# A graph network of three attention layers and an MLP layer: chunks of edges laid out by sixteen to a partition, turned on VectorE

## The reference, cut to what matters

```python
def _gat(x, edge_index, W, att_s, att_d, bias, heads, ch, neg_slope):
    h = (x @ W.T).reshape(n, heads, ch)
    a_s = (h * att_s[None]).sum(-1)
    a_d = (h * att_d[None]).sum(-1)
    logits = leaky_relu(a_s[src] + a_d[dst], neg_slope)
    m = segment_max(logits, dst)
    ex = exp(logits - m[dst])
    denom = segment_sum(ex, dst)
    alpha = ex / (denom[dst] + 1e-16)
    out = segment_sum(alpha[:, :, None] * h[src], dst)
    return out.reshape(n, heads * ch) + bias
# x = layernorm(x + gat3(elu_clip(gat2(elu_clip(gat1(x))))))
# the MLP layer:
    e_feat = concatenate([x[src], x[dst], edge_attr], axis=-1)
    v = relu(e_feat @ W1 + b1) @ W2 + b2
    x_cand = segment_max(v, dst)
# x = layernorm(x + maximum(x_cand, x))
```

## Time and profile before

| | |
|---|---|
| device time, median of 3 runs | 19831.58 us (19803.22 to 19836.53) |
| span of the profiled execution | 18272.2 us, 130521 instructions |
| that execution's time beyond its span | not given separately |
| busy in the span: PE, PEld | 8944.7 us (49%), 5685.5 us (31%) |
| busy: DVE, ACT, POOL | 6628.1 us (36%), 2818.0 us (15%), 13988.6 us (77%) |
| DMA | 655.33 MB, 36 GB/s over the span |

### The profile page before, as it was taken

The page is one execution under the profiler, slowest core; times in us unless marked ns, Lnnn a source line. Parts: engine busy times, 40 slices in busy tenths (PEclk is TensorE's granted clock), DMA queues, the critical chain, the costliest instruction groups (busy, mean ns, idle before and its releaser), DMA issues. The chain is left out here.

```text
span 18272.2 us, 130521 instructions
## 1 busy us (share of the span) xinstructions
PE 8944.7 (49%) x27930; PEld 5685.5 (31%) x27930; DVE 6628.1 (36%) x8375; ACT 2818.0 (15%) x6155; POOL 13988.6 (77%) x13430
## 2 busy tenths in 40 slices
PE   2444444444244444444424444444442566666664
PEld 1333333333133333333313333333331222222221
DVE  3444444344344444443434444444444211111113
ACT  3111111111111111111111111111111111111111
POOL 6777777777777777777777777777777777777776
PEclk9999999999999999999999999999999777777776
DMA  3111111111111111111111111111111222222221
GB/s 97 37 39 37 38 39 38 38 37 39 22 26 26 26 26 26 26 26 26 26 19 26 26 26 26 26 26 26 26 26 23 50 53 52 52 53 53 53 53 41
DMA packets 1418083, 655.33 MB, mean 36 GB/s; under 512 B 575697, under 2 KB 1396834, under 8 KB 1417732
## 3 DMA queue, kind: packets, MB, share of 16 engines
q1 hardware_dynamic: 984610, 414.51, 8.3%
q0 software_dynamic: 433440, 240.48, 7.5%
HBM read 361.76 MB, written 295.38 MB: 36 GB/s over the span
## 5 line engine op out<-in xcount | busy, mean ns | idle before, releaser
L591 POOL DMA_INDIRECT g<-table,idx x12512 | 13125.5, 1049 | 3813.7 <-issue 3731.7
L696 PE MATMUL bank<-adt_sb,ad_sel 32*128 32x128 f32 x4704 | 1200.5, 432 | 3525.8 <-DVE ph L1302 3524.0
L1285 DVE TENSOR_TENSOR u_sb<-adf,bank 128x512 f32<-128x512 f32 x588 | 404.2, 687 | 6931.2 <-PE bank L708 6931.2
L696 PEld LDWEIGHTS bank<-adt_sb,ad_sel 32*128 32x128 f32 x4704 | 1044.4, 323 | 3681.4 <-issue 3681.4
L704 PE MATMUL bank<-ident,g 128*128 128x128 f32 x2352 | 891.7, 456 | 2647.5 <-DMA g<-table,idx 2647.0
L722 PE MATMUL bank<-ident,mb 128*128 128x8 f32 x4704 | 1445.6, 381 | 0.0
L704 PEld LDWEIGHTS bank<-ident,g 128*128 128x128 f32 x2352 | 507.1, 245 | 2994.1 <-DMA g<-table,idx 2993.5
L708 PE MATMUL bank<-h_sb,w_as 128*128 128x512 f32 x1176 | 1217.8, 1139 | 447.5 <-ACT h_sb L805 447.5
L722 PE MATMUL bank<-ident,d_b 128*128 128x8 f32 x4704 | 1351.6, 361 | 0.2
L722 PEld LDWEIGHTS bank<-ident,mb 128*128 128x128 f32 x4704 | 1328.7, 331 | 0.0
L722 PEld LDWEIGHTS bank<-ident,d_b 128*128 128x128 f32 x4704 | 1328.0, 330 | 1.3 <-issue 1.3
(11 more groups left out here) (175 smaller groups left out, 9413.1 us busy)
## 6 DMA issues: line engine op xcount, KB each, us to landing
g<-table,idx POOLq DMA_INDIRECT x12512, 2.3
state<-o_sb SPq DMA_DIRECT2D x588, 288.0 KB, 2.4
auxx<-wide SPq DMA_DIRECT2D x98, 528.0 KB, 3.3
vmax<-o_sb SPq DMA_DIRECT2D x196, 256.0 KB, 2.4
lm<-auxx SPq DMA_DIRECT2D x98, 256.0 KB
lm<-in_edge_attr SPq DMA_DIRECT2D x392, 64.0 KB
dif<-auxx SPq DMA_DIRECT2D x98, 256.0 KB
dif<-in_edge_attr SPq DMA_DIRECT2D x391, 64.0 KB
```

The lines of the kernel that those rows point to most:

```text
L591: eng.indirect_dma_start(g[b][:, j * NQ + q, :], None, table[:, :], bass.IndirectOffsetOnAxis(ap=idx[b][:, q * J + j:q * J + j + 1], axis= ...
L696: last = eng.matmul(cols(p_ad, j), ad_sel[:, j, :], adt_sb[:, :], start=True, stop=True)
```

## The change

- The layout of a chunk: partition group q now holds quarter q of a chunk, with 16 consecutive edges (W = 16) on each of its 32 partitions (SQ = 32). A gathered buffer `g` is [128, 16, 32], and a 32x32 block turn inside each partition group brings it to feature by edge and back.
- VectorE makes these turns (`transpose`): four in an attention chunk (`tin` for `g`, `td` and `tm` for denominator and maximum, `ts` for the numerator), four in an MLP chunk (`txs`, `txd`, `txe`, `out`). The TensorE transposes, `p_h`, `p_s`, `p_dm`, `p_adt` and the copies out of them go.
- The target logits come from two matmuls with `ad` as it lies in DRAM (4 partitions), summed in `p_ad`.
- `lm`, the minimum and `dif` are made in place in a PSUM tensor `xw` of two banks; the first exponential stays there, the second goes to `pc`; `ph` is made in `xw` as well. `p_r` has two banks and the minimum reads it there.
- Four buffers of `idx` and `g` (NB = 4). POOL waits for the refilled indices alone. The loops run over 49 groups of four chunks. All chunks have 16 gathers, also the last two.
- SP stores each quarter by itself (4 DMAs a chunk), and loads target rows and edge features of the MLP by quarters (8).
- The indices are loaded from `src` straight into `idx_all` by five DMAs that ScalarE issues at the start; `srcp`, `st_` and their conversion, transposes and copies go.
- In an attention chunk VectorE's order becomes: logits of chunk n, turn and target scan of chunk n + 1, then the sums and turns of chunk n.

The diff, cut to its core:

```diff
-J = L // P
+SQ = 32
+W = L // SQ
+NB = 4
+NI = 196 // NB
...
-            def gather_edges(n, v, b, progress, k):
+            def gather_edges(n, k):
                 need(eng, S["aidx"], n + 1)
-                need(eng, progress, k)
                 tick(eng, "tickp")
-                for j in range(J):
-
-                    for q in range(NQ - 1 if isinstance(v, int) and v >= NC - 2 else NQ):
-                        eng.indirect_dma_start(g[b][:, j * NQ + q, :], None, table[:, :],
-                                               bass.IndirectOffsetOnAxis(ap=idx[b][:, q * J + j:q * J + j + 1], axis=0)).then_inc(e_g[b][j], 16)
+                for j in range(W):
+                    eng.indirect_dma_start(g[k][:, j, :], None, table[:, :],
+                                           bass.IndirectOffsetOnAxis(ap=idx[k][:, j:j + 1], axis=0)).then_inc(e_g[k][j // (W // 2)], 16)
...
+                    restart_row(b).then_inc(E["pr"], 1)
+                    need(eng, E["adf"], n)
+                    for h in range(2):
+                        last = eng.matmul(p_ad[:, :], ad_sel[:, h, :], view(ad[b], h, [[2, L]], parts=NQ), start=(h == 0), stop=(h == 1))
+                    last.then_inc(E["pad"], 1)
...
+            eng.wait_ge(S["edge"], 1)
+            for q in range(NQ):
+                n = N_SRC if q == NQ - 1 else NC
+                eng.dma_start(idx_all[q * SQ:(q + 1) * SQ, 0:n, :],
+                              bass.AP(tensor=I["src"].tensor, offset=q * Q, ap=[[W, SQ], [L, n], [1, W]])).then_inc(S["src"], 16)
...
+                def refill(i, k):
+                    v = i * NB + k
+                    need(eng, E["tin"], v + (layer * NC + 1))
+                    tick(eng, "ticks")
+                    next_idx(v, k)
+
+                def exps(i, k):
+                    n = i * NB + (layer * NC + k)
+                    need(eng, E["dif"], n + 1)
+                    eng.activation(xw[:, 0, :], xw[:, 0, :], ACT.Exp).then_inc(E["exp"], 1)
+                    eng.activation(pc[:, :], xw[:, 1, :], ACT.Exp).then_inc(E["exp"], 1)
...
+                def lead(i, k):
+                    b = k % 2
+                    n = i * NB + (layer * NC + k)
+                    for h in range(2):
+                        eng.wait_ge(e_g[k][h], gathered(layer, i))
+                    v_.transpose(view(h_sb[b], 0, [[1, W], [W, SQ]]), g[k][:, :, :]).then_inc(E["tin"], 1)
+                    need(eng, E["rs"], n + 1)
+                    need(eng, E["pad"], n + 1)
+                    need(eng, E["adf"], n)
+                    v_.tensor_tensor_scan(adf[b][:, :], r_sb[b][:, :], p_ad[:, :], adf[1 - b][:, L - 1:L], ALU.min, ALU.max).then_inc(E["adf"], 1)
+
+                def logits(i, k):
...
+                    v_.tensor_tensor(u_sb[:, :], adf[b][:, :], p_as[:, :], ALU.add).then_inc(E["u"], 1)
+                    need(eng, E["u"], n + 1)
+                    v_.scalar_tensor_tensor(xw[:, 0, :], u_sb[:, :], slope, u_sb[:, :], ALU.mult, ALU.max).then_inc(E["lm"], 1)
+                    v_.tensor_copy(mb[b][:, 0:1], mb[1 - b][:, L:L + 1]).then_inc(E["mbc"], 1)
...
+                    v_.tensor_tensor_scan(mb[b][:, 1:L + 1], r_sb[b][:, :], xw[:, 0, :], mb[b][:, 0:1], ALU.min, ALU.max).then_inc(E["mb"], 1)
+                    need(eng, E["mb"], n + 1)
+                    v_.tensor_tensor(xw[:, 1, :], mb[b][:, 0:L], p_r[b][:, :], ALU.min).then_inc(E["mn"], 1)
+                    need(eng, E["mn"], n + 1)
+                    v_.tensor_tensor(xw[:, :, :], xw[:, :, :], view(mb[b], 1, [[0, 2], [1, L]]), ALU.subtract).then_inc(E["dif"], 1)
+
+                def sums(i, k):
+                    v, b = i * NB + k, k % 2
+                    n = v + layer * NC
+                    need(eng, E["exp"], n * 2 + 2)
+                    v_.tensor_tensor_scan(d_b[b][:, :], pc[:, :], xw[:, 0, :], d_b[1 - b][:, L - 1:L], ALU.mult, ALU.add).then_inc(E["d"], 1)
+                    need(eng, E["d"], n + 1)
+                    v_.tensor_tensor(xw[:, 0, :], xw[:, 0, :], h_sb[b][:, :], ALU.mult).then_inc(E["ph"], 1)
+                    need(eng, E["ph"], n + 1)
+                    v_.tensor_tensor_scan(s_b[b][:, :], pc[:, :], xw[:, 0, :], s_b[1 - b][:, L - 1:L], ALU.mult, ALU.add).then_inc(E["s"], 1)
+                    need(eng, E["dm"], n)
+                    v_.transpose(dm_t[:, 0, :, :], view(d_b[b], 0, [[1, W], [W, SQ]])).then_inc(E["td"], 1)
+                    v_.transpose(dm_t[:, 1, :, :], view(mb[b], 1, [[1, W], [W, SQ]])).then_inc(E["tm"], 1)
+                    need(eng, E["s"], n + 1)
+                    need(eng, E[f"st{b}"], (v - b) * 32 + layer * NC * 32)
+                    v_.transpose(view(o_sb[b], 0, [[OW, W], [1, SQ]]), view(s_b[b], 0, [[1, W], [W, SQ]])).then_inc(E["ts"], 1)
...
+            def rows(v, b):
+                need(eng, M[f"ld{b}"], (v - b) * 72 + 144)
+                need(eng, M["adf"], v)
+                v_.transpose(view(p_xd, 0, [[1, W], [W, SQ]]), xd_in[b][:, :, :]).then_inc(M["txd"], 1)
+                need(eng, M["phid"], v * 2 - 2)
+                v_.transpose(view(xe_t[b], 0, [[1, W], [W, SQ]]), ea_in[b][:, :, :]).then_inc(M["txe"], 1)
...
+            def mlp(i, k, more=True):
+                v, b = i * NB + k, k % 2
+                for h in range(2):
+                    eng.wait_ge(e_g[k][h], gathered(3, i))
+                v_.transpose(view(xs_t[b], 0, [[1, W], [W, SQ]]), g[k][:, :, :]).then_inc(M["txs"], 1)
+                if more:
+                    rows(v + 1, 1 - b)
```

More of the change, by code:

```diff
@@ L103, in build @@
         wide = sb("wide", [P, 1617])
[L104 removed]
+        edge_i = sb("edge_i", [P, 27], i32)
         tail_f = sb("tail_f", [1, P])
@@ L411, in load_mlp @@
+                tick(eng, "tickl")
+                need(eng, M["txe"], v - 1)
+                tick(eng, "tickl")
                 ev = I["edge_attr_32"].rearrange("e f -> (e f)")
                 for q in range(NQ):
-                    rows = P
+                    part = slice(q * SQ, (q + 1) * SQ)
+                    eng.dma_start(xd_in[b][part, :, :].rearrange("c j f -> c (j f)"),
+                                  quarter(chunk_rows(auxx[0:EP, :], F), v, q)).then_inc(M[f"ld{b}"], 16)
+                    rows = SQ
@@ new lines, in source @@
+                def source(i, k):
+                    v, b = i * NB + k, k % 2
+                    n = v + layer * NC
+                    need(eng, E["tin"], n + 1)
+                    need(eng, E["u"], n)
+                    eng.matmul(p_as[:, :], w_as[layer][:, :], h_sb[b][:, :], start=True, stop=True).then_inc(E["pas"], 1)
+                front(0, 0)
+                front(0, 1)
+                source(0, 0)
+                for k in range(2, NB):
+                    front(0, k)
+                    source(0, k - 1)
@@ L743, in front @@
+                with eng.Fori(1, NI) as i:
+                    for k in range(NB):
+                        front(i, k)
+                        source(i - (k == 0), (k - 1) % NB)
+                source(NI - 1, NB - 1)
+            eng.wait_ge(E["dif"], 3 * NC)
             def front(v, b):
-                need(eng, M[f"ld{b}"], v * 48 + (96 - 48 * b))
-                need(eng, M["rs"], v)
+                need(eng, M[f"ld{b}"], (v - b) * 72 + 144)
+                need(eng, M["rs"], v - 1)
@@ new lines, in ends_out, with chunk @@
+                def ends_out(i, k):
+                    v, b = i * NB + k, k % 2
+                    n = v + layer * NC
+                    need(eng, E[f"st{b}"], (v - b) * 32 + layer * NC * 32)
+                    need(eng, E["tm"], n + 1)
+                    copy(view(o_sb[b], F, [[2, 2], [OW, W], [1, 2]]), view(dm_t, 0, [[W * SQ, 2], [SQ, W], [16, 2]])).then_inc(E["dm"], 1)
+                def chunk(i, k, more=True):
+                    exps(i, k)
+                    if more:
+                        refill(i if k + 1 < NB else i + 1, (k + 1) % NB)
+                        restart(i if k + 2 < NB else i + 1, (k + 2) % NB)
+                    ends_out(i, k)
@@ new lines, in _ @@
+                restart(0, 0)
+                restart(0, 1)
+                refill(0, 0)
+                for k in range(NB):
+                    chunk(0, k)
+                with eng.Fori(1, NI - 1) as i:
+                    for k in range(NB):
+                        chunk(i, k)
+                for k in range(NB - 2):
+                    chunk(NI - 1, k)
+                exps(NI - 1, NB - 2)
+                ends_out(NI - 1, NB - 2)
+                refill(NI - 1, NB - 1)
+                chunk(NI - 1, NB - 1, more=False)
@@ new lines, in chunk @@
+                def chunk(i, k):
+                    logits(i, k)
+                    lead(i if k + 1 < NB else i + 1, (k + 1) % NB)
+                    sums(i, k)
+                lead(0, 0)
+                for k in range(NB):
+                    chunk(0, k)
+                with eng.Fori(1, NI - 1) as i:
+                    for k in range(NB):
```

(12 more changed lines are left out.)

476 lines of the change are left out of this document (145 added, 331 removed).

## The result

The changed kernel takes 20214.79 us (median; 20148.88 to 20269.08), the kernel before in the same comparison 19832.19 (19803.22 to 19836.53). The ratio is 1.0193, with a 95% interval from 1.0171 to 1.0215: slower by 1.9% (no change lies outside the interval), where 18670 us, 5.9% faster, was forecast. The profiled execution took 20205.36 us, 1.8 us more than its span.

The account below looks back on a forecast made before the run. POOL's edge gathers were taken as the bound: 16939 us, 93% of the span. Terms -1258 + 112 - 14 - 3 = -1163 gave a span of 17109; with 1559.4 kept around it, about 18670 us, range 18470 to 19150.

Parts of the forecast that it names:

- The step that failed: Converting span to time: 1559.4 us between profiled span 18272.2 and median 19831.6, kept as a constant around the span.
- if the unshown 1559 us change by more than 100: A sign against the forecast: the difference between profiled span and timed median not staying constant within 100 us.
- SP: SP's extra stores and MLP loads, 0.4 to 0.5 us issue each: under 6 us of a 20 us chunk, costing nothing.
- three chunks of slack by four row buffers: POOL's four row buffers: worth 0, but covering any delay of the refill that now waits for tin.
- The gathers: POOL's gathers no longer held by VectorE: passes of 3136 x 1.250 = 3920.0 us, 15680 against 16938.2, -1258.
- the scale-and-max: VectorE's line 1287, still with two SBUF inputs: mean 0.19 us a chunk over 588 chunks, +112 us.
- The transposes: Four VectorE turns a chunk, taken at 0.7 us each: no cost beside the gathers unless they hold POOL.
- Rivals 1 and 2: VectorE's transposes hold POOL: at 0.7 us each +576, 19245, chance 0.15; at 1.4 us +2305, 20975, chance 0.05.
- Rival 3: Gather stretches come from something else in the chunk's rhythm, such as a transfer, and stay: about 19830, chance 0.03.
- Rival 4: VectorE binds a chunk: transposes of 3 us give 21.4 us a chunk, +820, 19490; chance 0.05.
- Tails and setup: Pass ends -3.5 us four times, -14; first node transpose earlier, -3; index loads 0, +15 as the bad end.
- The range: 18470 to 19150 us: all of the first case and rival 1's lower part; about 0.18 outside, slower 0.06.

Follow-up runs that it names:

- kind B: Comparisons in which the kernel before takes about 18155 us (18154 and 18157).
- kind A: Comparisons in which the kernel before takes 19.8 to 20.0 thousand us.
- before_again: The kernel before, unchanged, run with a trace of its own: 20000.93 us, span 19999.1.
- few_sbuf_2: Changed kernel with merged stores and MLP loads and xw in SBUF, run again in kind B: 18584.51 us, ratio 1.0234 to the kernel before.
- few_dmas: Changed kernel with one store a chunk for four and merged MLP loads (5 transfers a chunk, not 13): 19576.23 us, ratio 0.9794, kind A.
- sp_ticks: few_dmas with twelve more semaphore increments on SyncE before each attention store: 17207.56 us in kind B, 20775.31 in kind A.
- The fourth comparison: The changed kernel as it is (17198.62 us, ratio 0.9471) and few_sbuf_2 against the kernel before (18157.41 us).
- the fifth: sp_ticks (20775.31 us) and few_dmas with only the first hidden-layer product (19164.03 us); kernel before 19821.32 us.
- before_split: The kernel before with its one store a chunk split into four in all passes: 20051.15 us, ratio 1.0027, kind A.
- store_act: Changed kernel with the four stores of an attention chunk issued by ScalarE instead of SyncE: 19858.56 us (before 19968.61), kind A.
- few_act: few_dmas with the one attention store issued by ScalarE instead of SyncE: 19590.76 us, ratio 0.9785, kind A.
- one_store: Changed kernel with one store of 128 partitions in place of four, all passes, on SyncE: 19740.32 us, kind A.
- halves: few_dmas with the attention store as two transfers of 64 partitions, on SyncE and ScalarE: 17187.47 us, ratio 0.9469, kind B.
- few_sbuf: few_dmas with the tensor xw in SBUF instead of PSUM: 19677.21 us, ratio 0.9841, kind A.

## Why the prediction was wrong, point by point

**The step that failed** is the one that ties the span to the metric: "the median of the runs shown is 19831.6, so 1559.4 us lie around the span or are not shown by it. I keep them as a constant". An execution is 1.7 to 1.8 us longer than its span in all runs of the study. The 1559.4 us were the difference between the profiled execution, near kind B, and the timed ones of kind A. They lie inside the span: in before_again the passes are 1526 us longer than in the earlier trace rows and the rest of the span 200. In the passes they show as POOL's waits for the refill, 265.5 us in the second one and 891.9 in the MLP pass, the latter behind late results of TensorE. A page whose span is 8% below the median of the times isn't a page of those times, and the prediction said what would make it wrong ("if the unshown 1559 us change by more than 100") without asking what they are.

From there the numbers add up. The forecast was a span of 17109. In kind A the passes of the changed kernel are 18552.4 us where 15792 were forecast (15680 and 112): the gathers themselves sum to 11932, within 34 of the forecast's 11966, and the pauses to 6620 where 12544 x 0.305 = 3826 were expected, 2794 too many. Outside the passes it is 1651.2 for 1317, 334 too many. With 1558 less around the span that gives 20205.

**SP.** "Under 6 us of 20. No gather waits for them except at a pass end." In kind B this holds (POOL's idle time is all issue). In kind A it is the second failed term: 12.60 us for the four stores of the chunk shown, and 2354.8 us of POOL's waits end in the late refill (911.0 of them in the MLP pass). The cover that the argument named, three chunks of slack by four row buffers, is no cover here, since the loads of ad and r_in still have two buffers.

**The gathers: right.** Kind B has the forecast kernel: span 17195.7 for 17109. The timed gain there is 959 us (18157.41 to 17198.62), where 1163 were forecast: 87 are missing by the sum, and some 117 because the profiled execution of before was that much longer than those of kind B, which no trace explains. The MLP pass is 3914.7 (forecast 3920), the attention passes 3978.9 to 3981.6 (forecast "at most 135 us more" than 3920). The sum was 87 us short: the scale-and-max is hit in 432 of 588 chunks (they are all the stretched gathers of that trace), 65 us a pass more than the MLP pass and 195 in all, for 112 taken; outside the passes it is 1341.0 for 1317. Its read in the changed kernel, and the transposes beside it:

```profile
6441.17 1.03 DVE L1178 STREAM_TRANSPOSE h_sb<-g 128x512 f32<-128x512 f32 x1 [7.52 <-DMA g<-table,idx]
6441.31 0.94 POOL L593 DMA_INDIRECT g<-table,idx  x1 [0.30 <-issue]
...
6447.35 0.99 DVE L1212 STREAM_TRANSPOSE dm_t<-mb 128x512 f32<-128x512 f32 x1
...
6447.55 0.94 POOL L593 DMA_INDIRECT g<-table,idx  x1 [0.30 <-issue]
6448.27 0.99 DVE L1215 STREAM_TRANSPOSE o_sb<-s_b 128x512 f32<-128x512 f32 x1
...
6448.80 0.94 POOL L593 DMA_INDIRECT g<-table,idx  x1 [0.30 <-issue]
...
6449.58 1.86 SPq L320 DMA_DIRECT2D state<-o_sb  x4
6449.88 0.70 DVE L1191 SCALAR_TENSOR_TENSOR xw<-u_sb 128x512 f32<-128x512 f32 x1
6450.05 1.34 POOL L593 DMA_INDIRECT g<-table,idx  x1 [0.30 <-issue]
```

**The transposes** take 0.99 to 1.03 us, not 0.7, and 0.74 into PSUM. Rivals 1 and 2, that they hold POOL, are out: of 585, 582 and 582 gathers whose 0.125th us (the read instant of the prediction) falls inside the transposes of lines 1178, 1212 and 1215 in kind B, none is stretched. Rival 3 is out by few_sbuf_2: same rhythm, same transfers, xw in SBUF, 1374 us more. Worked out from the stretches of the earlier trace rows it was to be 1300 to 1550. The inference of the Trainium skill (SBUF — State Buffer, "Who interferes with whom") that descriptor generation isn't stalled falls with it: gathers of 1.74 us inside instructions with two SBUF inputs, 0.94 inside those with one. Rival 4 is out too: VectorE waits 7.52 us for its gathers in the chunk shown above.

**Tails and setup.** -14 and -3 were forecast. In kind B the stretches between passes are 281.6, 279.0 and 278.3 us, for 282.6, 280.9 and 280.2 before; the first gather starts at 330.8 for 321.5. Behind the last pass it is 171.3 for 168.8. So the tails between passes win 5 us, the last one loses 2.5, and the setup loses 9, inside the bad end that I gave; what delays it stays open.

**The range** left out the slower case but for 6%. The mechanism that made it was none of the rivals. By the trace of before alone it could not be priced, but it could be seen that the trace and the times disagreed by 1559 us.

## What to carry to other kernels

Before costing anything, hold the profile's span against the timed runs. If they differ by more than a few us, the profile is of another condition than the metric, and every "never waits" in it needs a margin. A change that speeds up the bounding engine by moving work into more instructions on a queue (three stores more a chunk here) should be costed at the slow end of that queue: here 12.60 us against 1.86 for the same four stores. Merging the transfers keeps a gain under both conditions: few_dmas 0.9794 in kind A; in kind B, where it wasn't run itself, sp_ticks, which is few_dmas with more increments, 17207.56 against 18153.93. That is the version to take.

## What the runs showed of the hardware that I had not expected

- The same program has two times. The kernel before takes 18154 and 18157 us in two comparisons and 19821 to 20004 in the others, with nothing between but the execution of about 18274 us of the first profile. The fourth comparison, of kind B, and the fifth, of kind A, carry the same chip number, so it isn't shown to be a property of the chip. In kind A, SyncE advances by 0.70 us a step for 2861 us of the kernel before, 13304 of the changed one, 6994 of few_dmas and 10574 of sp_ticks; in kind B for none of the changed kernel's span. In few_dmas 664 of the stretches between two waits of over 3 us hold such steps; in 609 of them they set in after three to seven quick instructions, and in 561 no quick instruction (under 0.3 us) follows before the next wait. before_split has nearly as many instructions on SyncE as the changed kernel and only 3919 us of such steps, so the number of instructions doesn't by itself bring the pace on. What does was not found.
- A rival that no run tests: the pace may be that of the recording, not of the kernel. Every timed execution here has its span on record, so none is known to have run unrecorded. In kind A most records of semaphore increments are missing from the traces, while those of instructions are as many as in kind B: 89935 increments for 285310 in the kernel before, 68308 for 323811 in the changed one. A pace that sets in after a few quick instructions and goes with a wait would fit something that fills up and empties. If it is the recording, kind B (0.947) is nearer to what the change is worth without it; an execution without recording would tell. It also means that in kind A's profiles who ended a wait ("remote" above all) is read from incomplete records, while the starts and lengths of instructions don't rest on them.
- Which engines have it depends on what they issue: ScalarE showed it only when it had the four stores (store_act), not with one (few_act). SyncE had it in every version of kind A, and POOL where it ran without pauses (1815 such steps in one_store, 1311 in few_dmas, 94 in the changed kernel).
- TensorE's results reach the waiting engines 9 to 25 us after the end shown in the MLP pass of kind A (17023.88 to 17032.90; 18623.86 to 18648.56). Ends of matmuls are modelled, so whether TensorE works later than shown or only reports later is open.
- It is not instruction fetching, as far as the queues show it. The Trainium skill (Runtime: NRT & Kernel Launch, "Instruction fetch mechanics") says that a taken branch to a target outside the window of two pages forces a fetch by DMA before execution goes on. The two instruction queues of the changed kernel moved 33 packets in the whole span of kind A, and the same 33 in kind B, so no run here shows such a stall:

```profile
q14 instruction: 30, 0.25, 0.0%
q8 instruction: 3, 0.05, 0.0%
```

- In kind A an attention chunk takes 22.3 us or more even where POOL never waits for a refill and no operand holds it (few_dmas, gathers of 1.09 to 1.12 us in a row). It is near 16 gathers at 1.40 us, 22.4, and POOL's own steps show that pace, but not all gathers have it (the commonest interval is still 1.25), so the floor isn't fully explained. It hides the operands' price: 101 us in kind A, 1374 in kind B. With xw in SBUF the attention passes are even the same in both kinds, 4430.1 to 4440.2 us in few_sbuf and 4432.0 to 4435.0 in few_sbuf_2; what kind A costs there lies in the MLP pass (4800.5 for 3914.2) and outside the passes. Whether a store in one piece of 128 partitions has a part in the floor was not settled, since halves fell in kind B.
